# Expert results shared out one step sooner, VectorE's own high part in half blocks, relational groups in pairs

## The chip, the cores and the metric

The kernel runs on one NeuronCore of a Trainium2 chip. Its engines run side by side, each with its own instruction list, and order themselves by semaphores: TensorE (PE in the profile; weight loads are PEld), VectorE (DVE), ScalarE (ACT), GpSimd (POOL) and SyncE (SP), which here only issues DMAs. The metric is the time of one execution on the device in microseconds (us). Three runs of the kernel before took 1425.64, 1419.89 and 1427.88 us.

## What is computed

The input x is 8192 tokens of 128 values (128 graphs of 64 nodes). Four residual layers, each on a layer norm of x, follow one another. Cut to what matters:

```
x = x + L0_gnn(layernorm(x), adj)        # 3 rounds of a gated graph network (GRU cell)
x = x + L0_ffn(layernorm(x))             # 8 experts, hidden 512, relu, top 2 of them
x = x + L1_gnn(layernorm(x), adj)        # relational graph convolution with a sigmoid gate
x = x + L1_ffn(layernorm(x))             # 8 experts, hidden 512, gelu, top 2 of them

def ffn(x):                              # both expert layers have this form
    top_p, top_e = top_2(softmax(x @ Wg + bg))
    for e in range(8):
        h = act(x @ W1[e] + b1[e])       # 128 -> 512
        y = h @ W2[e] + b2[e]            # 512 -> 128
        out += share(top_p, top_e, e) * y
```

## The kernel before

Stages follow one another: opening, gated graph (to about 470 us), first expert stage (names e1..., to about 806), relational stage (names c_..., to about 1058), second expert stage (names e2..., to about 1388), combine. Products in higher precision are split: a value is a high part in f16 and a low part in f16, and a product is three matmuls (lines L205, L206 and L207 of `passes`).

**Expert stages** (`experts`, L1381, called twice). Each token was sent to two slots of a table in DRAM (`slots`), sorted by expert, with a tag (home address, share). The table is worked off in 36 blocks of 512 slots: blocks 0 to 23 have one expert each (whole blocks), blocks 24 to 35 have two halves of 256 slots with an expert each (half blocks: each product and each bias is done twice on half the columns). Buffers come in rings of three (RING = 3). The hidden 512 values are four chunks of 128 (CH = 4). The work of block b:

- SP: `load(b)`, a transposing DMA of the block's rows into `xT`; `read_tags(b)`, a DMA of the tags into `label`. In iteration b of SP's loop it waits until up products of block b are done (`h_ps`), issues `load(b+3)` and then `read_tags(b+2)`, which waits for `homes`.
- TensorE: `up_c(b, c)`, chunk c of the hidden layer into one of four banks; `down_c(b, c)`, the product of chunk c with W2, summed up over the chunks; `turn(b)` (L1547), four transposes of the block's result back to rows.
- ScalarE: `hidden(c)` (L1586), the activation function from the bank into `hf` in f32; `hi(c)` (L1592), the high part of `hf` in f16 into `hs`. Its order is hidden0, hidden1, hi0, hidden2, hi1, hidden3, hi2, hi3.
- VectorE: `lo(c)` (L1605), the low part; `collect` (L1630), the sum of the down products out of the bank, with its bias; `addresses`, four small operations that make home addresses and shares for three blocks at once (L1617 to L1623); `share_out` (L1639), the transposed rows times their share into `ys`.
- GpSimd: four scatters (L1511, indirect DMAs) of a block's rows in `ys` to `results` in DRAM.

Each engine has its own order in a step b. TensorE: up(b+1, 0), down(b, 0), up(b+1, 1), down(b, 1), up(b+1, 2), down(b, 2), up(b+1, 3), down(b, 3), and `turn(b-1)` last. VectorE: collect(b-1); addresses, if b is the last of three; share_out(b-2); lo(b+1, 0) to lo(b+1, 3). After the last step VectorE still has collect(35), share_out(34), share_out(35). Blocks 3 to 20 run in a hardware loop (`Fori`) of three turns with six steps each; the others are written out. At block 2 of the first stage VectorE also makes MASK out of ADJ (L1660), two long operations.

**Relational stage** (`relational`, L1711). 16 groups of four tiles (512 tokens) go through a pipeline of 21 steps s. In step s TensorE turns over the tokens of group s-1 (`turn_a`) and the routing tokens of group s-4 (`turn_b`), makes the routing scores of group s-4 (`scores`), the values of group s-1 (`values`: per two tiles a bank, v = 0 and 1; biases are L1877), and the sums over the neighbours of group s-2. ScalarE copies the turned tokens out of the banks (`turned_a`, L1993, into `xT_a`; `turned_b`, L2006, into `xT_b`). VectorE empties the value banks (L2069), takes the scores in (`scores`, L2141) and chooses experts (`choose`) for a batch of groups. BATCHES says how: group 0, group 1 and then pairs, nine batches. `relational_sends` says how many rows of tokens GpSimd sends to their slots in each step, ahead of and behind its root (L1804), which it computes for the norms; ROUTED = 4 steps lie between a group's norm and its choice.

What VectorE's step looks like in the expert stages:

```
def step(b, j, i, v):
    if not isinstance(b, int) or b:
        collect(b - 1, 1 - v)
    if j == RING - 1:
        addresses(b - j, i)
    if not isinstance(b, int) or b > 1:
        share_out(b - 2, (j - 2) % RING, i - (j < 2), v)
    for c in range(CH):
        if not last(b):
            lo(b + 1, (j + 1) % RING, c)
```

## Time and profile before

| | before |
|---|---|
| median of three runs | 1425.64 us (1419.89 to 1427.88) |
| the profiled execution | 1428.36 us, its span 1426.6 us |
| TensorE busy | 918.1 us (64%), 5850 instructions |
| VectorE busy | 905.9 us (64%), 2456 instructions |
| ScalarE busy | 765.8 us (54%), 1392 instructions |
| GpSimd busy | 733.9 us (51%), 717 instructions |
| granted TensorE clock, mean | 0.787 of full speed |

No engine is busy over two thirds of the span, so the stages have to be read one by one, and in a stage one step by itself: how long it lasts, which engine is never idle in it, and which wait ends last. The chain that the profile follows back from the last instruction stays within the last 2% of the span (combine) and says nothing of the stages.

### The profile page before, as it was taken

The numbers are of one execution on the slowest core, as the hardware profiler recorded it, in microseconds if no ns is written. First come the engines' busy times: TensorE is split into PE (matmuls) and PEld (weight loads), VectorE is DVE, ScalarE is ACT, GpSimd is POOL, SyncE is SP. The second block draws the span as 40 slices with busy tenths as digits, with TensorE's granted clock in tenths as the row PEclk, the third lists the DMA queues.
The fourth block names the chain that finished last, engine by engine and source line by source line (L and its number), as shares of the span: only waits on it lengthen the run. The fifth ranks groups of instructions, "written<-read, shape, count | busy, mean of one in ns | idle before, by whom it ended". The sixth has DMA issues, their size and how long they took to land. (4 is left out here: it accounts for less than half of the span.)

```text
span 1426.6 us, 23103 instructions
## 1 busy us (share of the span) xinstructions
PE 918.1 (64%) x5850; PEld 519.1 (36%) x5851; DVE 905.9 (64%) x2456; ACT 765.8 (54%) x1392; POOL 733.9 (51%) x717
## 2 busy tenths in 40 slices
PE   2368778888862357888787176656432968888820
PEld 1244344444432123434565133323210433346620
DVE  5967799999985345555544367767642645554626
ACT  2476767677762145666565165656431655666710
POOL 3501132876757646556544416567566444655540
PEclk9579999999995679899988555555556998999955
DMA  9233221221201524424221223321131342333209
GB/s 249 90 127 94 77 46 23 59 61 48 59 22 42 136 58 100 91 67 85 64 50 45 71 90 119 104 65 55 32 62 52 87 105 58 84 67 70 61 28 340
DMA packets 199164, 115.62 MB, mean 81 GB/s; under 512 B 155084, under 2 KB 175710, under 8 KB 198528
## 3 DMA queue, kind: packets, MB, share of 16 engines
q1 hardware_dynamic: 169008, 69.54, 20.8%
q0 software_dynamic: 17408, 34.13, 7.4%
q10 hardware_dynamic: 12624, 10.49, 2.8%
q8 instruction: 54, 0.88, 0.3%
q14 instruction: 70, 0.57, 0.1%
HBM read 43.80 MB, written 51.61 MB: 67 GB/s over the span
## 5 line engine op out<-in xcount | busy, mean ns | idle before, releaser
L644 POOL DMA_INDIRECT slots<-ROWS,pos x256 | 265.4, 1037 | 78.5 <-issue 71.4
L1511 POOL DMA_INDIRECT results<-e1ys,e1home x144 | 155.5, 1080 | 136.1 <-DVE e1ys L1639 93.7
L1511 POOL DMA_INDIRECT results<-e2ys,e2home x144 | 151.1, 1049 | 136.2 <-DVE e2ys L1639 93.0
L1586 ACT ACTIVATE e1hf<-psum,VT 128x512 f32<-128x512 f32 (+1 forms) x192 | 104.3, 583 | 151.6 <-PE psum L207 82.0
L1605 DVE SCALAR_TENSOR_TENSOR e1hs<-e1hf,e1hs 128x512 f16<-128x512 f32 x144 | 95.6, 690 | 127.4 <-ACT e1hs L1592 88.9
L1586 ACT ACTIVATE e2hf<-psum,VT 128x512 f32<-128x512 f32 (+1 forms) x192 | 104.8, 582 | 126.0 <-remote 59.1
L1605 DVE SCALAR_TENSOR_TENSOR e2hs<-e2hf,e2hs 128x512 f16<-128x512 f32 x144 | 95.8, 691 | 112.5 <-ACT e2hs L1592 83.0
L1363 POOL TENSOR_TENSOR a_Z<-a_Z,a_H 128x512 f32<-128x512 f32 x48 | 68.2, 1420 | 161.5 <-ACT a_Z L1093 159.2
L205 PE MATMUL psum<-e2hs,W 128*128 128x512 f16 (+1 forms) x192 | 66.7, 347 | 55.9 <-DVE e2hs L1605 25.9
L205 PE MATMUL psum<-a_hT,WHH 128*128 128x512 f16 x144 | 58.8, 408 | 52.5 <-ACT a_Z L1093 48.3
L205 PE MATMUL psum<-e1xT,W 128*128 128x512 f16 (+1 forms) x192 | 67.6, 352 | 38.5 <-DMA e1xT<-slots 16.7
L205 PE MATMUL psum<-e1hs,W 128*128 128x512 f16 (+1 forms) x192 | 67.4, 351 | 35.8 <-DVE e1hs L1605 24.9
L1592 ACT ACTIVATE e1hs<-e1hf 128x512 f16<-128x512 f32 x144 | 86.9, 631 | 0.0
L1592 ACT ACTIVATE e2hs<-e2hf 128x512 f16<-128x512 f32 x144 | 86.7, 631 | 0.0
L205 PE MATMUL psum<-e2xT,W 128*128 128x512 f16 (+1 forms) x192 | 66.7, 348 | 23.4 <-issue 11.0
L1804 POOL TENSOR_TENSOR c_rs<-c_var,mhalf 128x12 f32<-128x12 f32 (+2 forms) x22 | 40.5, 1843 | 79.9 <-DVE c_var L2082 45.1
L207 PE MATMUL psum<-e1xT,W 128*128 128x512 f16 (+1 forms) x192 | 67.7, 353 | 3.3 <-issue 3.2
L206 PE MATMUL psum<-e1hs,W 128*128 128x512 f16 (+1 forms) x192 | 67.5, 352 | 2.7 <-issue 1.7
L206 PE MATMUL psum<-e1xT,W 128*128 128x512 f16 (+1 forms) x192 | 67.5, 351 | 2.7 <-issue 2.7
L207 PE MATMUL psum<-e1hs,W 128*128 128x512 f16 (+1 forms) x192 | 67.4, 351 | 2.7 <-issue 2.5
L207 PE MATMUL psum<-e2xT,W 128*128 128x512 f16 (+1 forms) x192 | 66.5, 346 | 1.6 <-issue 1.5
L206 PE MATMUL psum<-e2xT,W 128*128 128x512 f16 (+1 forms) x192 | 66.5, 346 | 0.4 <-issue 0.4
(363 smaller groups left out, 2643.6 us busy)
## 6 DMA issues: line engine op xcount, KB each, us to landing
c_G<-results SPq DMA_DIRECT2D x32, 256.0 KB
d_G<-results SPq DMA_DIRECT2D x32, 256.0 KB, 5.2
slots<-slots SPq DMA_DIRECT2D x16, 264.0 KB
W<-in_L_ffn_W_dram SPq DMA_DIRECT2D x16, 256.0 KB, 3.4
kept<-a_cut SPq DMA_DIRECT2D x16, 256.0 KB, 2.6
slots<-ROWS,pos POOLq DMA_INDIRECT x256
W<-kept SPq DMA_DIRECT2D x8, 512.0 KB
out_dram<-X ACTq DMA_DIRECT2D x16, 256.0 KB, 7.1
```

Of the source, the lines that this page charges most:

```text
L205: pe.matmul(out, lhs(0), rhs(0), start=start, stop=False, skip_group_check=True)
L206: pe.matmul(out, lhs(0), rhs(1), start=False, stop=False, skip_group_check=True)
L207: return pe.matmul(out, lhs(1), rhs(0), start=False, stop=stop, skip_group_check=True)
L644: pool.indirect_dma_start(out=slots, out_offset=bass.IndirectOffsetOnAxis(ap=k["pos"][:, c, t:t + 1], axis=0), in_=k["ROWS32"][:, t, :], i ...
L1363: pool.tensor_tensor(Z[p % 2][:, :], Z[p % 2][:, :], H[p][:, :], ALU.mult).then_inc(zh_sb, 1)
L1511: pool.indirect_dma_start(out=k["results"][m], out_offset=bass.IndirectOffsetOnAxis(ap=home[:, GT * b + q:GT * b + q + 1], axis=0), in_=ys ...
L1586: t = act.activation(hf[c][:, cols], HB[c][:, cols], func, bias=VT[:, bass.ds(e * CH + b1_col + c, 1)], scale=1 / PS)
L1592: act.activation(hs[j][:, 0, c, :], hf[c][:, :], ACT.Copy, scale=AS).then_inc(h_hi, 1)
L1605: dve.scalar_tensor_tensor(out=hs[j][:, 1, c, :], in0=hf[c][:, :], scalar=AS, in1=hs[j][:, 0, c, :], op0=ALU.mult, op1=ALU.subtract).then_ ...
L1804: pool.tensor_tensor(rstd[s % 4][:, lo:hi], var[s % 2][:, lo:hi], k["mhalf"][:, lo:hi], ALU.pow)\
```

## The change

Three parts.

In both expert stages TensorE does `turn(b-1)` in the middle of step b, behind down(b, 1); VectorE does `share_out(b-1)` in step b, between the low parts of chunks 1 and 2, in place of share_out(b-2) at the step's start; `addresses` comes at the second block of each three, not the third; and SP reads the tags of block b+2 before it waits to load block b+3.

In the steps that prepare half blocks VectorE makes the high part of the last chunk itself (`own_high`, a `tensor_scalar` with its own semaphore), and ScalarE leaves it out. `his_by` counts ScalarE's high parts accordingly.

In the relational stage all groups are routed in pairs (eight batches); sends to the slots start one step later, with eight rows a step; TensorE makes the values of a group's first two tiles (v = 0) ahead of the scores; and ScalarE's turned_b stands ahead of norms_a.

```diff
@@ -1408,6 +1408,7 @@
         y_stored = k["stored"][m]
         h_ps, h_f32, h_hi, h_lo, yT_ps, yT_sb, y_ps, y_sb = (
             sem(n) for n in ("h_ps", "h_f32", "h_hi", "h_lo", "yT_ps", "yT_sb", "y_ps", "y_sb"))
+        own_hi = sem("own_hi")
         counted, listed, tails, match, weight, homes, second_in = (
             sem(n) for n in ("counted", "listed", "tails", "match", "weight", "homes", "second_in"))
         HB = banks[0:4]
@@ -1435,6 +1436,13 @@
             if isinstance(b, int) and b >= FULL:
                 return [(2 * b - FULL + h, slice(h * HALF, (h + 1) * HALF)) for h in range(2)]
             return [(b, slice(0, BLK))]
+
+        def halved(b):
+            return isinstance(b, int) and b >= FULL
+
+        def his_by(b):
+
+            return CH * (b + 1) - (max(0, b + 1 - FULL) if isinstance(b, int) else 0)
 
         def half_rows(buf, h):
             return buf[:, :, :].rearrange("p s n -> p (s n)")[:, h * BLK:(h + 1) * BLK].rearrange("p (s n) -> p s n", s=2)
@@ -1488,6 +1496,8 @@
                     sp.wait_ge(counted, 1)
                 if RING <= b < RING + E:
                     tail(b - RING)
+                if 1 <= b and b + 2 < NBLK:
+                    read_tags(b + 2, rows.pop(b + 2))
                 if b + RING == EARLY:
                     sp.wait_ge(listed, 1)
                     sp.wait_ge(tails, 16 * E)
@@ -1495,8 +1505,6 @@
                 if b + RING < NBLK:
                     sp.wait_ge(h_ps, 4 * b + 4)
                     rows[b + RING] = load(b + RING)
-                if 1 <= b and b + 2 < NBLK:
-                    read_tags(b + 2, rows.pop(b + 2))
 
         @block.gpsimd
         def _(pool):
@@ -1568,8 +1576,8 @@
                         known[:] = [e, who(b + 2)]
                     elif c == 1:
                         known[:] = [e, None]
-                if not isinstance(b, int) or b:
-                    turn(b - 1, 1 - v)
+                    if c == 1 and (not isinstance(b, int) or b):
+                        turn(b - 1, 1 - v)
             rounds(pe, step)
             turn(NBLK - 1, (NBLK - 1) % 2)
 
@@ -1595,13 +1603,23 @@
                 for c in range(1, CH):
                     hidden(c)
                     hi(c - 1)
-                hi(CH - 1)
+                if not halved(b):
+                    hi(CH - 1)
             rounds(act, step)
 
         @block.vector
         def _(dve):
+            def own_high(b, j):
+                c = CH - 1
+                dve.wait_ge(h_f32, CH * (b + 1))
+                dve.tensor_scalar(hs[j][:, 0, c, :], hf[c][:, :], AS, None, ALU.mult).then_inc(own_hi, 1)
+                dve.wait_ge(own_hi, b - FULL + 1)
+
             def lo(b, j, c):
-                dve.wait_ge(h_hi, 4 * b + c + 1)
+                if halved(b) and c == CH - 1:
+                    own_high(b, j)
+                else:
+                    dve.wait_ge(h_hi, his_by(b - 1) + c + 1)
                 dve.scalar_tensor_tensor(out=hs[j][:, 1, c, :], in0=hf[c][:, :], scalar=AS, in1=hs[j][:, 0, c, :],
                                          op0=ALU.mult, op1=ALU.subtract).then_inc(h_lo, 1)
 
@@ -1647,13 +1665,13 @@
             def step(b, j, i, v):
                 if not isinstance(b, int) or b:
                     collect(b - 1, 1 - v)
-                if j == RING - 1:
+                if j == 1:
                     addresses(b - j, i)
-                if not isinstance(b, int) or b > 1:
-                    share_out(b - 2, (j - 2) % RING, i - (j < 2), v)
                 for c in range(CH):
                     if not last(b):
                         lo(b + 1, (j + 1) % RING, c)
+                    if c == 1 and (not isinstance(b, int) or b):
+                        share_out(b - 1, (j - 1) % RING, i - (j < 1), 1 - v)
                 if m == 0 and isinstance(b, int) and b == RING - 1:
                     for h in range(2):
                         half = slice(h * NODES, (h + 1) * NODES)
@@ -1661,8 +1679,7 @@
             rounds(dve, step)
             end = NBLK - 1
             collect(end, end % 2)
-            for b in (end - 1, end):
-                share_out(b, b % RING, b // RING, b % 2)
+            share_out(end, end % RING, end // RING, end % 2)
 
 
 
@@ -1681,16 +1698,16 @@
         sp.dma_start(G[:, c, :, :], rows[:, c, bass.ds(GT * g, GT), :]).then_inc(sem, 16)
 
 
-BATCHES = [(0, 1), (1, 1)] + [(g, 2) for g in range(2, 16, 2)]
+BATCHES = [(g, 2) for g in range(0, 16, 2)]
 ROUTED = 4
 SPLIT = 6
 
 
 def relational_sends(NG):
 
-    first = ROUTED + 1
+    first = ROUTED + 2
     n = NG + ROUTED + 1
-    wanted = [0 if s < first else (8, 6, 2)[s - first] if s < first + 3 else 8 if s < NG else CARRY for s in range(n)]
+    wanted = [0 if s < first else 8 if s < NG else CARRY for s in range(n)]
     early = 2 * GT * (NG - QUAD)
     return [max(min(w, early - sum(wanted[0:s])), 0) for s, w in enumerate(wanted)]
 
@@ -1865,11 +1882,10 @@
                 pe.wait_ge(lo_a, g + 1)
                 turn_over(TAh, tok_a[p]).then_inc(a_ps, 1)
 
-            def values(g, p):
+            def values(g, p, v):
 
                 pe.wait_ge(a_sb, g + 1)
-                for q in range(GT):
-                    v = q // 2
+                for q in range(2 * v, 2 * v + 2):
                     if q % 2 == 0:
                         wait_from(pe, val_sb, 2 * g + v - 1)
                     o = Vv[v][:, q % 2, :, :].rearrange("p s d -> p (s d)")
@@ -1939,10 +1955,12 @@
                     turn_a(s - 1, (s - 1) % 2)
                 if 0 <= s - 4 < NG:
                     turn_b(s - 4)
+                if 0 <= s - 1 < NG:
+                    values(s - 1, (s - 1) % 2, 0)
                 if 0 <= s - 4 < NG:
                     scores(s - 4)
                 if 0 <= s - 1 < NG:
-                    values(s - 1, (s - 1) % 2)
+                    values(s - 1, (s - 1) % 2, 1)
                 if 0 <= s - 2 < NG:
                     neighbours(s - 2, s % 2)
                 b, g, n = chosen_at(s)
@@ -2008,10 +2026,10 @@
             def step(s):
                 if 0 <= s - 1 < NG:
                     turned_a(s - 1, (s - 1) % 2)
+                if 0 <= s - 4 < NG:
+                    turned_b(s - 4)
                 if s < SPLIT:
                     norms_a(s, s % 2)
-                if 0 <= s - 4 < NG:
-                    turned_b(s - 4)
                 if 0 <= s - 2 < NG:
                     v_his(s - 2, s % 2)
                 if SPLIT <= s < NG:
```

## Rows read from the trace of the kernel before

**Rows 1.** Windows, two of each expert stage: us, busy time of each engine, PEclk, DMA

```profile
534.00:683.00 149.00, 122.44 (x572) 57.27 (x573) 86.07 (x152) 92.94 (x164) 87.34 (x81) 0.94 0.39 85
683.00:788.00 105.00, 82.78 (x605) 62.99 (x604) 50.55 (x99) 59.94 (x137) 50.70 (x48) 0.86 0.25 52
1120.00:1276.00 156.00, 126.00 (x575) 58.09 (x574) 83.60 (x148) 93.70 (x164) 84.09 (x80) 0.91 0.35 81
1276.00:1369.00 93.00, 74.50 (x603) 59.93 (x601) 50.97 (x98) 60.42 (x138) 50.57 (x48) 0.92 0.29 62
```

**Rows 2.** Table of waits: engine, line, releaser: us in total, times, longest us

```profile
ACT e2hf L1586 <- remote: 59.1, 14, 14.3
ACT e1hf L1586 <- remote: 57.3, 13, 11.6
```

**Rows 3.** Timeline of a whole step, second stage: start us, us, instruction

```profile
1155.73 0.38 PE L207 MATMUL psum<-e2xT,W 128*128 128x512 f16 x1
...
1156.60 0.60 PE L1547 MATMUL psum<-identf,e2yT 128*128 128x128 f32 x4
1157.04 0.38 PE L205 MATMUL psum<-e2xT,W 128*128 128x512 f16 x1
...
1159.41 0.38 PE L207 MATMUL psum<-e2hs,W 128*128 128x512 f16 x1
...
1161.35 0.38 PE L207 MATMUL psum<-e2xT,W 128*128 128x512 f16 x1
...
1156.25 0.69 ACT L1586 ACTIVATE e2hf<-psum,VT 128x512 f32<-128x512 f32 x1
1156.84 1.14 ACT L1592 ACTIVATE e2hs<-e2hf 128x512 f16<-128x512 f32 x2
...
1157.49 1.29 DVE L1605 SCALAR_TENSOR_TENSOR e2hs<-e2hf,e2hs 128x512 f16<-128x512 f32 x2 [0.53 <-ACT e2hs L1592]
1158.91 0.75 DVE L1630 TENSOR_SCALAR e2yT<-psum,VT 128x512 f32<-128x512 f32 x1
```

**Rows 4.** Timeline of a half step, first stage

```profile
737.27 0.27 PE L207 MATMUL psum<-e1xT,W 128*128 128x256 f16 x1
...
740.98 0.27 PE L207 MATMUL psum<-e1hs,W 128*128 128x256 f16 x1
...
741.04 0.88 DVE L1630 TENSOR_SCALAR e1yT<-psum,VT 128x256 f32<-128x256 f32 x2 [0.67 <-issue]
```

**Rows 5.** Groups by line and form, VectorE: busy us, mean ns of one | idle

```profile
L451 DVE TENSOR_SCALAR WIH<-W 128x384 f16<-128x384 f32 x3 | 1.1, 352 | 0.0
```

**Rows 6.** Timeline at MASK in the first expert stage

```profile
530.01 2.65 POOL L1511 DMA_INDIRECT results<-e1ys,e1home  x1 [0.30 <-issue]
...
530.26 4.58 DVE L1660 TENSOR_SCALAR MASK<-ADJ 64x4096 f16<-64x4096 int32 x2
```

**Rows 7.** Timeline, GpSimd, end of the second expert stage: first and last of twelve

```profile
1370.80 0.98 POOL L1511 DMA_INDIRECT results<-e2ys,e2home  x1 [7.49 <-DVE e2ys L1639]
...
1384.92 0.98 POOL L1511 DMA_INDIRECT results<-e2ys,e2home  x1 [0.31 <-issue]
```

**Rows 8.** Timeline of relational step 10

```profile
929.85 1.02 ACT L1993 ACTIVATE c_xT_a<-psum 128x1024 f16<-128x1024 f16 x1 [4.47 <-remote]
...
929.97 0.75 DVE L2069 SCALAR_TENSOR_TENSOR c_sg<-psum,c_sg 128x256 f32<-128x256 f32 x2
...
931.85 0.19 PE L205 MATMUL psum<-WGATE,c_xT_b 128*128 128x8 f16 x1 [4.44 <-ACT c_xT_b L2006]
...
932.26 0.60 PE L1877 MATMUL psum<-relbias,ones 1*128 1x256 f16 x2
...
934.83 0.60 PE L1877 MATMUL psum<-relbias,ones 1*128 1x256 f16 x2
```

**Rows 9.** Waits of VectorE, relational stage, 854 to 1053 us

```profile
DVE S L2141 <- PE psum L207: 20.3, 10, 3.3
```

**Rows 10.** Groups of VectorE, 850.8 to 854.4 us: one of the routing operations

```profile
L585 DVE TENSOR_TENSOR v_wide<-revidx,ROWS 128x32 f32<-128x32 f32 x1 | 0.2, 193 | 0.0
```

## The prediction

> **What bounds the kernel now.** I read the time per stage first, then one undisturbed step of each kind in the timeline, then the table of waits. The two expert stages are the part that the change rewrites most. Cut at the last down product of a block, the 20 whole-block steps 4 to 23 take 149 us in the first expert stage and 156 us in the second, 7.45 and 7.8 us a step; the 12 half-block steps 24 to 35 take 105 and 93 us, 8.75 and 7.75 us a step [rows 1]. TensorE is busy for 80 to 82% of them and is the engine with most to do, but an undisturbed step is shorter than these means: in the timeline [rows 3] chunk 3 of block 8 is up-projected at 1155.73 and the next one at the same place comes 5.62 us later (1161.35), which is the four transposes' 0.44 us and eight groups of products, one up or down product of a chunk each, at 0.645. The rest are pauses: ScalarE waits 57.3 and 59.1 us, in 13 and 14 pieces, for a releaser that the profile can't name [rows 2]. So an expert step is 5.6 us of TensorE work plus, in some steps, a pause of 4 us or so. GpSimd, with 4 scatters of about 1.28 us (start to start [rows 7]) a block, has room to spare, except at the end of a stage: there 12 scatters stand one behind the other, from 1370.80 to 1385.90.
>
> In the relational stage VectorE sets the pace; what it waits for most is the score product of TensorE, 20.3 us in 10 waits [rows 9].
>
> **Moved transposes and share_out, whole blocks.** TensorE now does turn(b-1) in the middle of step b, behind down(b, 1), and not at its end. Nothing is added to its work, but the transposes wait for collect(b-1), and behind them in TensorE's order stand up(b+1, 2), down(b, 2), up(b+1, 3) and down(b, 3). When does collect finish? The timeline shows the chain of an undisturbed step [rows 3]: the last up product ends at 1155.73 + 0.38 = 1156.11; ScalarE makes the activation (start 1156.25) and then both high parts (end 1157.98), VectorE both low parts (end 1158.78), and collect ends at 1158.91 + 0.75 = 1159.66, which is 3.55 us after the product. In the old order TensorE passes down(8, 1) at 1159.79, so nothing would show. But the transposes (0.44 us, 1156.60 to 1157.04) are no longer ahead of it, so TensorE is there at 1159.35. It waits for collect: 0.31 us, plus about 0.13 for the semaphore (the gap between the product's end and ScalarE's start in this step, 1156.11 to 1156.25). The step becomes a loop of 3.55 + 0.13 + 0.44 + three groups of products at 0.645 = 6.05 us in place of 5.62: plus 0.43. There are 22 such steps in a stage (1 to 22), so 9.5 us. Below, 0, if every one has its slack from elsewhere; above, 1 us a step where ScalarE is still behind after a pause.
>
> **Half blocks, with the high part on VectorE.** The same chain [rows 4]: product end 737.27 + 0.27 = 737.54, collect end 741.04 + 0.88 = 741.92, so 4.38 us, while down(30, 1) ends at 740.98 + 0.27 = 741.25. The old order thus would be 0.67 us short by itself. own_high takes some 0.6 us (of the 1.14 for two high parts [rows 3]) off ScalarE, which isn't last here, and puts a tensor_scalar 128x512 to f16 on VectorE between low parts 2 and 3. No such operation is in the trace; the nearest is the 128x384 at 0.352 us [rows 5], so 0.35 to 0.47 us; I take 0.42, and 0.1 for VectorE's wait on its own semaphore. The two low parts run back to back (1.29 us for both [rows 3]), so it adds its length to the chain: 4.90. Between the ends 737.54 and 741.25 lie the transposes and five groups, 0.654 each; an undisturbed half step is thus 0.44 + 8 x 0.654 = 5.67, and the new loop 4.90 + 0.13 + 0.44 + 3 x 0.654 = 7.4 us: plus 1.75, in 11 steps 19 us. Without own_high it would be plus 1.2. Bounds: 0 (a pause covers it) to 2.4.
>
> A 2-port operation of VectorE can also hold up GpSimd: a scatter that meets the MASK operation takes 2.65 us, not 0.98 [rows 6, 7]. 12 operations of 0.42 us a stage are at most 5 us of GpSimd's time, and GpSimd idles in the half steps; only where it is last would it count, and none of them falls behind the last block. Cost zero. The Trainium skill has this as a rule that speaks against the edit (page "SBUF — State Buffer", section "SBUF: two separate sides": a VectorE operation in a 2-port mode locks GpSimd out of the shared ports, so that it can't write descriptors); by that rule, the trace agrees, and if every lock were on the path the sum would be 10 us longer over both stages, which the idle time in the rows of GpSimd contradicts.
>
> **How much of it shows.** 9.5 + 19 = 28.5 us a stage, 57 for both. 27 of the 70 steps hold a pause [rows 2]. Where the pause falls behind the new place of the transposes, the wait lies inside it. I take half of them so: 57 x (1 - 27/140) = 46 us.
>
> **The end of a stage.** Here the change gains. share_out(33) is done in step 34 and share_out(34) in the middle of step 35, so of the 12 scatters that stood behind the last blocks only 8 are left: 4 x 1.28 = 5.1 us a stage, 10.3 for two. Bounds 0 (if the last steps come later by as much) and 2 x 10.
>
> **Addresses and tag reads.** The four small operations move from step j = 2 to j = 1 of each three, and SP reads the tags of block b+2 before it waits for h_ps, no longer behind the load. SP's order is load, tags, load, tags as before; the one tag read in three that waits for `homes` now stands ahead of the load of one block sooner, and its release comes one step sooner too. The load still has two steps. Zero; if SP came late, up(b+3) would wait: at most 1 us in every third step, 20 us.
>
> **Relational stage.** (a) values for tiles 0 and 1 now go ahead of the scores on TensorE. In step 10 [rows 8] xT_a is there at 929.85 + 1.02 = 930.87 and VectorE has emptied the bank (first of the two value operations from 929.97 on) at about 930.4; the half takes 932.26 to 934.83 = 2.57 us. The scores (0.41 us, 931.85 to 932.26) start not at 931.85 but at 930.95 + 2.57 = 933.5. VectorE waits for them in order, with choose, the shifts and the next mixture queued behind. Its wait per step is 2.57 + 0.41 + 0.3 for two semaphores less its second value operation 0.4 = 2.9 us; in the 13 steps 4 to 16 that have both, 37 us against 20.3 before: plus 17. VectorE has other waits that this can swallow; I take plus 12, between 0 and 20. (b) One routing batch fewer: 19 small operations at about 0.19 us [rows 10] go, and those of the first pair grow by some 0.03 us each: minus 3.0. GpSimd sends 8 and 8 rows in steps 6 and 7, not 6 and 2, and a root stands behind: plus 2.6 at most. I take minus 1.5. (c) turned_b ahead of norms_a acts in steps 4 and 5 alone: zero, within 1 us.
>
> **Sum.** The profiled execution took 1428.4 us, with a span of 1426.6; the median of the runs is 1425.6, 2.7 less. 1428.4 + 46 - 10.3 + 12 - 1.5 = 1474.6, and on the scale of the median 1472.
>
> **Rivals.** *The pauses set the pace* (the one on the other side, not slower). Steps last 7.45 to 8.75 us on average, the new loops 6.05 and 7.4. If the pauses come because TensorE runs at 5.6 us a step, a slower step has fewer of them, and the expert stages keep their length. For: the pauses come once in two to three steps, after fast ones. Against: in the trace a step with a pause is longer by the whole pause, and the next is 5.6 us again. It decides once the pauses shrink by 46 us out of 116. Time: 1425.6 - 10.3 + 12 - 1.5 = 1426; with the wait for scores swallowed too, 1414. *The relational order pays and the chain doesn't bind*: TensorE idles for xT_b in the old order, and with 2.57 us of work put there its own chain to relu is 1 us shorter in 13 steps. With the tails: 1425.6 - 10.3 - 13 - 1.5 = 1401. Against: VectorE, not TensorE, is last there. *Every wait shows in full, with ScalarE behind after pauses*: 1 us in whole steps and 2.2 in half ones, 2 x (22 + 24) = 92: 1425.6 + 92 - 10.3 + 15 = 1522. *The change doesn't do what it says*: scatters of block b-1 would not start before step b+1 if the transposes came so late that share_out slips; then the tails stay and 1482 results.
>
> **Chances.** Forecast, with tails kept or lost, 1440 to 1508: 0.54. Full waits, above 1508: 0.07. Pauses set the pace, 1419 to 1440, most of it within 0.5%: 0.20. Faster (scores swallowed as well, 0.10, or the relational order pays, 0.09): 0.19. 0.5% is 7 us, about what a measurement of this kernel can tell from no change: 1418.5 to 1432.8. So faster 0.20, same 0.16, slower 0.64, the last with the upper end of the pauses' case. The range leaves out the full waits and the faster half of the faster cases: 1412 to 1508; the likeliest case by itself spans 1445 to 1500.
>
> **What would show it.** Right: TensorE idle before its transposes (L1547), released by VectorE's collect, some 0.4 us in whole and over 1 us in half steps; the undisturbed whole step at 6.0 us, the half one at 7.4; VectorE's wait for the scores near 2.9 us in each of 13 steps; 8 scatters behind the last share_out but one. Wrong: steps of 5.6 us still there, or a sum of pauses well under 116 us with expert stages as long as before.

## The result, and the profile after

The changed kernel takes 1448.5 us (median of six runs, 1442.2 to 1455.2), the kernel before beside it 1429.7 us: a ratio of 1.0188, with a 95% interval of 1.0133 to 1.0242. (Ratios leave out runs more than 1.5% above the fastest of the same kernel, so they need not be the quotient of the medians.) So it is slower, by 19 us by the medians and 27 by the ratio; 1472 had been forecast, with 1412 to 1508 as the range. Its profiled execution took 1447.9 us, with a span of 1446.1 (1426.6 before).

The span cut into stages, an expert stage from its first up product to the end of its last scatter, and the relational stage as what lies between the two (each cut read from the timeline of its profile):

| us | before | after | difference |
|---|---|---|---|
| opening and gated graph | 477.2 | 477.2 | 0.0 |
| first expert stage | 327.1 | 322.8 | -4.3 |
| relational stage | 258.7 | 283.4 | +24.7 |
| second expert stage | 322.9 | 322.8 | -0.1 |
| combine | 40.7 | 39.9 | -0.8 |
| span | 1426.6 | 1446.1 | +19.5 |

I had put plus 46 on the longer expert steps, minus 10 on the ends of the expert stages and plus 10 or so on the relational stage. The sign of the total is right, its size is too large, and the places are wrong.

Windows of the changed kernel, cut where those of [rows 1] are, at the last down products of blocks 3, 23 and 35 of each expert stage (us, busy time of each engine, PEclk, DMA share, GB/s):

```profile
547.00:690.00 143.00, 125.32 (x577) 58.51 (x576) 82.94 (x148) 93.84 (x162) 86.62 (x80) 0.94 0.37 85
690.00:791.00 101.00, 73.26 (x596) 60.95 (x594) 55.06 (x111) 54.76 (x124) 49.40 (x50) 0.94 0.26 54
1147.00:1289.00 142.00, 122.54 (x573) 57.19 (x572) 83.29 (x148) 94.50 (x163) 85.72 (x79) 0.96 0.38 85
1289.00:1396.00 107.00, 77.30 (x603) 63.00 (x600) 56.23 (x111) 54.11 (x124) 51.92 (x49) 0.92 0.26 52
```

Whole steps have a mean of 7.15 and 7.1 us, where it was 7.45 and 7.8; half steps 8.4 and 8.9, where it was 8.75 and 7.75. Yet the undisturbed step did become longer, as forecast. The timeline in the second stage, from the transposes of block 9 to those of block 10:

```profile
1193.35 0.66 PE L1555 MATMUL psum<-identf,e2yT 128*128 128x128 f32 x4 [0.38 <-DVE e2yT L1648]
...
1195.57 0.38 PE L207 MATMUL psum<-e2xT,W 128*128 128x512 f16 x1
...
1196.08 0.69 ACT L1594 ACTIVATE e2hf<-psum,VT 128x512 f32<-128x512 f32 x1
1196.67 1.14 ACT L1600 ACTIVATE e2hs<-e2hf 128x512 f16<-128x512 f32 x2
...
1197.38 1.28 DVE L1623 SCALAR_TENSOR_TENSOR e2hs<-e2hf,e2hs 128x512 f16<-128x512 f32 x2
1198.74 0.75 DVE L1648 TENSOR_SCALAR e2yT<-psum,VT 128x512 f32<-128x512 f32 x1
...
1199.54 0.66 PE L1555 MATMUL psum<-identf,e2yT 128*128 128x128 f32 x4 [0.36 <-issue]
```

The product ends at 1195.95, collect at 1199.49, 3.54 us later (forecast 3.55, [rows 3]), and TensorE is idle ahead of its transposes until then (0.36 to 0.38 us). The step is 6.19 us (1193.35 to 1199.54), against 5.62.

What gave the time back stands in the table of waits, whole span:

```profile
PE psum L1555 <- DVE e1yT L1648: 52.3, 27, 12.0
DVE S L2159 <- PE psum L207: 39.9, 15, 3.4
PE psum L1555 <- DVE e2yT L1648: 30.0, 21, 3.1
ACT e2hf L1594 <- remote: 21.9, 4, 15.6
```

The first and third lines are the forecast waits of TensorE for collect. The last answers to [rows 2]: ScalarE's waits for a releaser that isn't named have gone from 59.1 us in 14 pieces to 21.9 in 4 (in the first stage from 57.3 in 13 to 10.1 in one). The second line is VectorE's wait for the scores, 21.7 us before over the same whole span.

An unnamed wait is only one name under which a pause shows. The 12.0 us in the first line ended at 520.73, just behind one of ScalarE's unnamed waits (10.06 us, to 517.12): in the new order TensorE, too, is made to wait by a pause, and under the name of collect. So 116.4 to 32.0 us tells that the pauses became fewer, not by how much; the comparison of the two kinds of chip below does.

Another wait in that line was not in the forecast. In block 2 of the first stage VectorE makes MASK, and collect stands behind it; now the transposes and half of TensorE's step stand behind collect:

```profile
535.07 4.75 DVE L1678 TENSOR_SCALAR MASK<-ADJ 64x4096 f16<-64x4096 int32 x2
539.84 0.75 DVE L1648 TENSOR_SCALAR e1yT<-psum,VT 128x512 f32<-128x512 f32 x1
...
540.72 1.11 PE L1555 MATMUL psum<-identf,e1yT 128*128 128x128 f32 x4 [5.72 <-DVE e1yT L1648]
```

The end of the second expert stage, GpSimd and VectorE (L1648 is collect, L1657 share_out; the first and the last scatter of twelve):

```profile
1390.60 1.45 POOL L1519 DMA_INDIRECT results<-e2ys,e2home  x1 [4.48 <-DVE e2ys L1657]
...
1405.23 0.98 POOL L1519 DMA_INDIRECT results<-e2ys,e2home  x1 [0.31 <-issue]
...
1396.69 0.88 DVE L1648 TENSOR_SCALAR e2yT<-psum,VT 128x256 f32<-128x256 f32 x2 [1.34 <-PE psum L207]
1398.31 0.69 DVE L1657 TENSOR_TENSOR e2ys<-psum,e2share 128x512 f32<-128x512 f32 x1 [0.75 <-issue]
```

From the last collect to the end of the last scatter it is 1396.69 to 1406.21, 9.5 us. Before, the last collect stood at 1370.79, and the last scatter [rows 7] ended at 1385.90: 15.1 us. The gain of 5.6 us is close to the 5.1 of the forecast.

### The profile page after: what moved, and what is told of

Same layout as the page of the kernel before. It is cut to its first block and busy times, and to the rows that moved or that the text cites. A ratio compares the mean times of both kernels' runs of the same rounds, so it can differ in the third digit from the quotient of the medians.

```text
span 1446.1 us, 23094 instructions
## 1 busy us (share of the span) xinstructions
PE 917.6 (63%) x5849; PEld 525.9 (36%) x5850; DVE 912.3 (63%) x2461; ACT 758.3 (52%) x1366; POOL 732.3 (51%) x717
## 3 DMA queue, kind: packets, MB, share of 16 engines
q1 hardware_dynamic: 169008, 69.54, 20.3%
## 5 line engine op out<-in xcount | busy, mean ns | idle before, releaser
L644 POOL DMA_INDIRECT slots<-ROWS,pos x256 | 261.8, 1023 | 78.4 <-issue 72.0
L1519 POOL DMA_INDIRECT results<-e2ys,e2home x144 | 154.1, 1070 | 133.1 <-DVE e2ys L1657 90.7
L1600 ACT ACTIVATE e2hs<-e2hf 128x512 f16<-128x512 f32 x132 | 80.0, 625 | 0.0
L1600 ACT ACTIVATE e1hs<-e1hf 128x512 f16<-128x512 f32 x132 | 79.8, 623 | 0.0
L205 PE MATMUL psum<-e1hs,W 128*128 128x512 f16 (+1 forms) x192 | 66.5, 347 | 11.2 <-issue 4.2
L206 PE MATMUL psum<-e1hs,W 128*128 128x512 f16 (+1 forms) x192 | 66.2, 345 | 0.0
L207 PE MATMUL psum<-e1hs,W 128*128 128x512 f16 (+1 forms) x192 | 65.7, 342 | 0.0
```

The lines of the kernel that those rows point to most:

```text
L205: pe.matmul(out, lhs(0), rhs(0), start=start, stop=False, skip_group_check=True)
L206: pe.matmul(out, lhs(0), rhs(1), start=False, stop=False, skip_group_check=True)
L207: return pe.matmul(out, lhs(1), rhs(0), start=False, stop=stop, skip_group_check=True)
L644: pool.indirect_dma_start(out=slots, out_offset=bass.IndirectOffsetOnAxis(ap=k["pos"][:, c, t:t + 1], axis=0), in_=k["ROWS32"][:, t, :], i ...
L1519: pool.indirect_dma_start(out=k["results"][m], out_offset=bass.IndirectOffsetOnAxis(ap=home[:, GT * b + q:GT * b + q + 1], axis=0), in_=ys ...
L1600: act.activation(hs[j][:, 0, c, :], hf[c][:, :], ACT.Copy, scale=AS).then_inc(h_hi, 1)
```

## Experiments

Theory A: the loss comes from the split values, which hold back the scores; and in the expert stages something hides the longer steps. Its rivals are in the expectations. The first four kernels ran beside a kernel before of 1427.7 us (median of 19 runs, which lie between 1405.1 and 1455.8).

### The relational edits one by one

r_split is the kernel before with one edit:

```diff
-                if 0 <= s - 4 < NG:
-                    scores(s - 4)
                 if 0 <= s - 1 < NG:
-                    values(s - 1, (s - 1) % 2)
+                    values(s - 1, (s - 1) % 2, 0)
+                if 0 <= s - 4 < NG:
+                    scores(s - 4)
+                if 0 <= s - 1 < NG:
+                    values(s - 1, (s - 1) % 2, 1)
```

> The kernel before with one edit of the relational stage alone: the values of a group's first two tiles ahead of the scores. Theory A (the delayed scores, with VectorE standing in wait for them, are the loss): 15 to 25 us slower, the relational stage near 280 us from the last scatter of the first expert stage to the first up product of the second, in place of 259, and VectorE's wait for the scores above 30 us. Rival B (the loss comes from the pairs and the later sends): within 5 us of before. My term for this edit was plus 12, bounds 0 and 20.

1452.5 us, a ratio of 1.0244 (1.0129 to 1.036), as theory A has it. The relational stage is 274.2 us, 15.5 more than before. Its line in the table of waits:

```profile
DVE S L2142 <- PE psum L207: 44.7, 15, 6.1
```

r_pairs is the kernel before with the routing in pairs:

```diff
-BATCHES = [(0, 1), (1, 1)] + [(g, 2) for g in range(2, 16, 2)]
+BATCHES = [(g, 2) for g in range(0, 16, 2)]
-    first = ROUTED + 1
-    wanted = [0 if s < first else (8, 6, 2)[s - first] if s < first + 3 else 8 if s < NG else CARRY for s in range(n)]
+    first = ROUTED + 2
+    wanted = [0 if s < first else 8 if s < NG else CARRY for s in range(n)]
```

> The kernel before with the eight batches of pairs and the sends that go with them, and nothing else. Theory A: minus 1.5 us by my sum, within 4 us of before. Rival B (routing or the sends, now one step later, hold the stage up): 10 us or more slower.

1439.0 us, 1.0156 (1.0039 to 1.0273). By the total alone, 11.3 us over the median beside it, this is rival B. But in its profile the relational stage is 260.1 us, 1.4 more than before, and the one stage that is clearly longer is the second expert stage, which this edit doesn't touch (333.8 us against 322.9, half steps at 8.3 us and not 7.75). r_split, which doesn't touch it either, shows 333.0 there. All four runs of r_pairs also lie between the lowest and the highest of the kernel before. An expert stage can thus differ by 10 us where its code is the same, and the total of one edit of this size can't be read on it; the stage can. Two later kernels with the pairs in them bear this out: r_unsplit below is no slower than e_all, and best, on the other chip, has a relational stage of 242.8 us against 242.3.

e_all is the kernel before with the whole expert part and no relational edit; r_unsplit is the changed kernel with `values` in one piece behind the scores again.

> The kernel before with the whole of the expert part (transposes behind down(b, 1), share_out one step sooner, addresses and tag reads sooner, VectorE's high part in half blocks) and the relational stage untouched. Forecast by my sum: 46 - 10 = plus 36 us. Theory A (undisturbed steps are longer, as forecast, but the pauses shrink by as much): between minus 10 and plus 5 us, with undisturbed whole steps at 6.2 us and not 5.6.

> The changed kernel with one edit undone: all values behind the scores again. Theory A: 15 to 25 us faster than the changed kernel, so 1420 to 1430, level with before or a little under it. Rival B: still 1440 or more. If the edits of the stages are independent, its time is that of the expert part alone and of the pairs alone, added.

e_all: 1422.5 us, 1.0034 (0.9985 to 1.0083). r_unsplit: 1419.95 us, 1.0008 (0.996 to 1.0055). Both medians are 5 to 8 us under that of the kernel before, both ratios a little over 1. So about 28 us of the changed kernel's time go with the one edit (28.5 against its own median, which is from another series of runs; 26 by the difference of the ratios), and the expert part, for which my sum says plus 36, costs nothing that can be measured. If the pairs really cost the 11 us of r_pairs, r_unsplit would stand at 1434; it doesn't. In r_unsplit's profile the relational stage is 254.3 us; in the changed kernel's it is 283.4.

How the edit works is seen in one step of the changed kernel (timeline; L2024 is the copy into xT_b, L2087 VectorE's emptying of a value bank, L1893 the value biases, L2159 the scores on VectorE):

```profile
954.69 1.02 ACT L2024 ACTIVATE c_xT_b<-psum 128x1024 f16<-128x1024 f16 x1
...
955.08 0.75 DVE L2087 SCALAR_TENSOR_TENSOR c_sg<-psum,c_sg 128x256 f32<-128x256 f32 x2
...
955.64 0.58 PE L1893 MATMUL psum<-relbias,ones 1*128 1x256 f16 x2 [5.25 <-DVE c_sg L2087]
...
958.05 0.21 PE L205 MATMUL psum<-WGATE,c_xT_b 128*128 128x8 f16 x1
...
958.60 0.19 DVE L2159 TENSOR_TENSOR S<-psum,c_rs 128x32 f32<-128x32 f32 x1 [2.77 <-PE psum L207]
```

xT_b is there at 955.71, and in the old order the scores would follow at once, as in [rows 8]. Now TensorE first makes values of two tiles, which in turn had to wait for VectorE to empty their bank (xT_a was there at 954.79, TensorE begins at 955.64); the scores start at 958.05, and VectorE, which has had nothing to do since 955.83, stands in wait for 2.77 us. 15 such waits make 39.9 us, 2.66 each.

### The expert edits one by one, on another chip

Four kernels: e_tags is the kernel before with `addresses` at j == 1 and the tag reads ahead of the wait for the load; e_noown is the expert part without own_high; best is the changed kernel with unsplit values and with the transposes and share_out moved to the end of the step; e_turn0 is the expert part with them moved further forward. best and e_turn0 differ from the changed kernel in this place (3 in best, as shown, and 0 in e_turn0, in place of 1):

```diff
-                    if c == 1 and (not isinstance(b, int) or b):
+                    if c == 3 and (not isinstance(b, int) or b):
                         turn(b - 1, 1 - v)
...
-                    if c == 1 and (not isinstance(b, int) or b):
+                    if c == 3 and (not isinstance(b, int) or b):
                         share_out(b - 1, (j - 1) % RING, i - (j < 1), 1 - v)
```

> The kernel before with two small edits of the expert stages alone: addresses at the second block of each three, and the tag reads ahead of the wait for the next load. The transposes stay at the end of TensorE's step and share_out is that of block b-2. I had these at zero. Theory C (the earlier addresses take the wind out of the pauses, and that has paid for the longer steps of the expert part): 30 to 50 us faster than before, undisturbed steps at 5.62 us, ScalarE's waits for a releaser not named well under 116 us. Rival D (the pauses shrink because TensorE's steps are longer): within 6 us of before, pauses as before.

> The expert part without VectorE's high part: transposes behind down(b, 1), share_out, addresses and tags sooner, ScalarE makes all four high parts. My sum: half steps 0.55 us shorter than with it in 11 steps of each stage, so 12 us faster than the whole expert part (1422.5), about 1410. Theory D (something else sets the mean step): within 4 us of the whole expert part, with shortest half steps at 6.9 us, not 7.7.

> The changed kernel without the split values and with the transposes back at the end of TensorE's step (share_out of block b-1 behind the last low part, so 8 scatters are left at the end of a stage, as in the changed kernel). Against the changed kernel with unsplit values (1419.95). My sum says the longer steps cost 46 us in both stages: 1375 to 1395. Theory C: the same, 1375 to 1400. Theory D: 1412 to 1426, with undisturbed whole steps at 5.62 us and pauses as long as before the change.

> The expert part with the transposes still sooner, behind down(b, 0), and share_out behind the first low part. The loop through collect then holds five groups of products: 3.55 + 0.13 + 0.44 + 5 x 0.645 = 7.35 us for an undisturbed whole step, and about 8.7 for a half one. If each longer step shows in full: 22 x 1.3 + 11 x 1.3 = 43 us a stage more than the whole expert part, 1510. Theory D (a mean of 7.2 to 7.5 us for whole steps is set elsewhere): whole steps stay near 7.5 us, half ones near 8.7, together 10 us a stage more at most, 1420 to 1445.

They ran on another chip than the four above, and there the kernel before itself takes 1229.0 us (19 runs, 1226.6 to 1232.6), 200 us less. All absolute numbers expected above therefore miss, and what they were to decide about the pauses (theories C and D) can't be read here; the ratios can:

| kernel | us | ratio to before there |
|---|---|---|
| e_tags | 1229.4 | 1.0008 (0.9994 to 1.0021) |
| best | 1230.1 | 1.0001 (0.9988 to 1.0015) |
| e_noown | 1279.2 | 1.0403 (1.0381 to 1.0425) |
| e_turn0 | 1424.3 | 1.1593 (1.1568 to 1.1617) |

On this chip the pauses don't exist. The windows of e_tags, blocks 4 to 23 and 24 to 35 of the second stage:

```profile
987.00:1099.00 112.00, 112.00 (x571) 57.19 (x570) 84.25 (x148) 96.36 (x164) 87.34 (x80) 1.00 0.48 108
1099.00:1167.00 68.00, 66.19 (x599) 57.92 (x597) 48.02 (x96) 59.92 (x135) 53.06 (x50) 1.00 0.44 85
```

20 whole steps take 112 us, 5.62 each without an exception, TensorE is busy for all of it, and the clock is granted in full; in [rows 1] the same 20 steps take 156 us at 0.91. The table of waits of this kernel has no line with a releaser that isn't named. With no pauses to hide it, the place of the transposes shows in full. TensorE's transposes of e_noown in the half steps of the first stage:

```profile
702.74 0.66 PE L1547 MATMUL psum<-identf,e1yT 128*128 128x128 f32 x4 [1.16 <-DVE e1yT L1630]
...
709.79 0.66 PE L1547 MATMUL psum<-identf,e1yT 128*128 128x128 f32 x4 [1.16 <-DVE e1yT L1630]
```

That is 7.05 us a half step, with 1.16 us of waiting for collect. Whole steps are 6.19 us in e_noown and 7.49 in e_turn0 (expected 7.35), half ones about 10.5 in e_turn0, where I had expected 8.7. The clock is enough to explain the missing 1.8 us: TensorE stands idle for 3 us in each of these steps, and then 15 to 23 of its products run at a granted clock of 0.50 and start 0.1 us further apart. The half steps of the first stage as a whole, one wait for collect, and two stretches of the step that follows it (windows: PEclk is the third number from the right):

```profile
677.00:801.00 124.00, 87.35 (x595) 69.04 (x593) 55.77 (x109) 54.00 (x122) 49.16 (x49) 0.82 0.20 42
732.85 1.11 PE L1554 MATMUL psum<-identf,e1yT 128*128 128x128 f32 x4 [3.37 <-DVE e1yT L1647]
735.30:738.60 3.30, 3.30 (x17) 2.37 (x16) 1.29 (x2) 2.02 (x5) 0.00 (x0) 0.50 0.02 5
738.80:741.50 2.70, 2.70 (x26) 2.26 (x24) 1.03 (x2) 2.15 (x5) 0.98 (x1) 1.00 0.07 24
```

In the slow stretch a product of 256 columns starts every 0.21 us, in the fast one every 0.11. e_noown, whose waits are 1.16 us, keeps a clock of 0.98 to 1.00 in its half steps. My sum for a longer wait had no term for this.

e_noown is 50.2 us slower than the kernel before, from the place of the transposes and of share_out alone (e_tags, with the moved addresses and tags, is level). best has the steps back at 5.62 and the shorter stage ends, and is still no faster: its half steps are 5.85 and 6.05 us on average, against 5.7 in e_tags, two whole steps of its second stage are longer too, and together they eat up the gain at the stage's end (12.6 us from the last collect to the last scatter's end, against 17.2 and 18.4). Which of its edits lengthens the half steps wasn't tried; own_high is one of them.

### The changed kernel on both kinds of chip

> The changed kernel once more, because the kernel before took 1229 us beside the last four kernels and 1428 us beside the first four. On a chip where the kernel before takes about 1229 us and shows no pauses, the longer steps must show in full: whole steps 6.2 in place of 5.62 in 22 steps (13 us a stage), half steps near 7.8 in place of 5.7 in 11 steps (23 us), the tails minus 5 a stage, the split values plus 16 to 29: plus 78 to 91 us, 1307 to 1320. On one where it takes about 1428 us: 1440 to 1455 as measured.

> The whole expert part with the relational stage untouched, once more beside the changed kernel. Where the kernel before takes about 1229 us: 2 x (13 + 23 - 5) = plus 62, 1291. Where it takes about 1428 us: 1415 to 1430 as measured. The difference to the changed kernel is the relational part on the same chip: 16 to 29 us on either.

> The changed kernel with unsplit values and the transposes back at the end of TensorE's step, which was level with before (1230.1 against 1229.0) on a chip where undisturbed steps fill the stages. Where the kernel before takes about 1430 us: Theory D says 1412 to 1430, since what sets the mean step there isn't the chain through collect; my first sum says 1375 to 1395, because the longer steps should show.

> The changed kernel, beside the last. Where the kernel before takes about 1229 us: 1307 to 1320, as expected before. Where it takes about 1430 us: 1440 to 1455.

The first two ran beside a kernel before of 1431.3 us (13 runs, 1412.5 to 1452.5). whole: 1448.9 us, 1.0166 (1.0131 to 1.0201). e_all_again: 1417.1 us, 0.9881 (0.9814 to 0.9948). So the relational edits cost 31.8 us there, a little above the 16 to 29 expected, and the expert part is faster than the kernel before, by 14 us by the medians and 17 by the ratio. With e_all, which was level, that makes 0 to 1.2% for the same kernel.

The other two ran beside one of 1227.4 us, so best_again could not tell what the old place of the transposes, with the shorter stage ends, brings where there are pauses. best_again: 1230.4 us, 1.0022 (1.0012 to 1.0033). whole_again: 1306.1 us, 1.0624 (1.0598 to 1.065): plus 78.7 us, where 78 to 91 had been worked out from the measured steps. Its table of waits, and the half steps of the first stage with own_high (L1615):

```profile
DVE S L2159 <- PE psum L207: 39.3, 15, 2.8
PE psum L1555 <- DVE e1yT L1648: 37.0, 36, 5.0
PE psum L1555 <- DVE e2yT L1648: 33.1, 35, 3.0
```

```profile
701.49 0.42 DVE L1615 TENSOR_SCALAR e1hs<-e1hf 128x512 f16<-128x512 f32 x1
...
703.41 0.88 DVE L1648 TENSOR_SCALAR e1yT<-psum,VT 128x256 f32<-128x256 f32 x2 [0.77 <-issue]
...
704.34 0.66 PE L1555 MATMUL psum<-identf,e1yT 128*128 128x128 f32 x4 [1.70 <-DVE e1yT L1648]
...
711.92 0.66 PE L1555 MATMUL psum<-identf,e1yT 128*128 128x128 f32 x4 [1.69 <-DVE e1yT L1648]
```

A half step is 7.58 us, 0.53 more than without own_high (7.05), with the operation itself at 0.42.

The same kernels on both kinds of chip, stage by stage (each from its profile, steps from the last down product of one block to that of another; for the kernel before on the second kind stands e_tags, which is level with it; none: without pauses):

| us | old steps, pauses | changed, pauses | old steps, none | changed, none |
|---|---|---|---|---|
| mean whole step, stage 1 / 2 | 7.45 / 7.8 | 7.15 / 7.1 | 5.73 / 5.62 | 6.3 / 6.35 |
| mean half step, stage 1 / 2 | 8.75 / 7.75 | 8.4 / 8.9 | 5.7 / 5.7 | 7.55 / 7.45 |
| undisturbed whole step | 5.62 | 6.19 | 5.62 | 6.19 |
| first expert stage | 327.1 | 322.8 | 238.9 | 274.3 |
| relational stage | 258.7 | 283.4 | 242.3 | 254.2 |
| second expert stage | 322.9 | 322.8 | 235.4 | 264.7 |

Without pauses, the expert part costs 35.4 + 29.3 = 64.7 us and the relational part 11.9. With pauses, the expert part costs nothing or gains up to 17, and the relational part costs 25 to 32.

Read across, the table says what the pauses are worth with all that hangs on them: the two expert stages are 88.2 + 87.5 = 175.7 us longer with pauses in the old order, and 48.5 + 58.1 = 106.6 us in the new one. The pauses thus gave back 69 us, where the steps took 65.

## Why the prediction was right, and where it wasn't

**What bounds an expert step.** That an undisturbed step is 5.6 us of TensorE and the rest is pauses was right, and the chip without pauses shows it: 5.62 us a step. What I took for the kernel's own nature, though, belongs to the chip on which it ran. And a pause costs more than the time in which TensorE stands still: TensorE is busy for 126 us in the 20 whole steps of the second stage [rows 1] and for 112 in e_tags, with the same products. So of 44 us, 14 are products at a lower granted clock (0.91 against 1.00), and 30 are idle time.

**Moved transposes.** The chain through collect was right to 0.01 us (3.54 against 3.55), the loop short by 0.14 (6.19 against 6.05): the last up product's row ends 0.16 us after the next product starts (0.38 against the 0.22 from start to start in the timeline), and I had counted the step from starts and the chain from that end. As I had it, 22 x 0.43 = 9.5 us a stage; with the measured step 22 x 0.57 = 12.5.

**Half blocks.** own_high at 0.42 us was right, and so was its place on the chain: 0.53 us a step measured against 0.52 worked out (4.90 against 4.38). The half step is 7.58 us (the terms of the forecast add up to 7.43), without own_high 7.05 (6.91): the same 0.14 to 0.15 again. That ScalarE has one operation less in the step buys nothing: own_high's cost shows in full. Its operations were taken as free for GpSimd, and nothing speaks against that: the scatters take 1.08 and 1.07 us on average in the two stages, 1.08 and 1.05 before.

**How much of it shows: the step that failed.** I took 57 us, less a share of 27/140 for steps in which a pause would cover the wait, 46, which with the ends of the stages is plus 36. The profile with pauses showed minus 4 instead, the one without pauses plus 65. The discount assumed pauses that stay as they are while a wait hides inside some of them. In fact they shrank by about what the steps grew, 69 us against 65. The unnamed waits of ScalarE in the expert stages tell the same of every kernel that ran on a chip with pauses: 116 to 123 us in the three with old steps (the kernel before, r_split, r_pairs), 23 to 51 in the five with the expert part. The rival that I gave 0.20, *the pauses set the pace*, is what happened in these expert stages, and the pauses passed the point of decision that I had named (a loss of 46 of 116 us). Its reason, that pauses come because TensorE runs at 5.6 us a step, isn't shown: on the other chips e_tags runs at 5.62 us a step and has none.

What the pauses are stays open. The trace of the kernel before shows one in the second stage so (ScalarE, the weight loads and the products of TensorE):

```profile
1140.34 0.69 ACT L1586 ACTIVATE e2hf<-psum,VT 128x512 f32<-128x512 f32 x1 [2.49 <-PE psum L207]
1148.59 0.69 ACT L1586 ACTIVATE e2hf<-psum,VT 128x512 f32<-128x512 f32 x1 [7.56 <-remote]
...
1138.64 0.38 PE L207 MATMUL psum<-e2xT,W 128*128 128x512 f16 x1
...
1142.75 0.10 PEld L207 LDWEIGHTS psum<-e2xT,W 128*128 x1
1150.62 0.10 PEld L205 LDWEIGHTS psum<-e2hs,W 128*128 x1 [7.78 <-issue]
```

The product for which ScalarE waits (chunk 1 of block 7) stands at 1138.64, but ScalarE goes on only at 1148.59; by then TensorE has run out of work too. GpSimd's scatters go on through it. The profile models the ends of products, so it can't tell whether they were finished late or whether the word of them came late. The DMA traffic of the kernel is the same on both kinds of chip (199164 packets, 115.62 MB), so it isn't by itself the cause; whether it takes part on the one kind wasn't tried. Why kernels with longer TensorE steps have less of them isn't shown either, only that they do: five profiles with 6.2 us steps have mean whole steps of 7.0 to 7.4 us, three with 5.6 us steps 7.45 to 7.8. All five also have the earlier addresses, tag reads and share_out; which of these edits shrinks the pauses wasn't taken apart where there are pauses. I can't say from this that a mean of about 7.3 us would hold for other loops: e_turn0, meant to show it, ran where there are no pauses.

**The end of a stage.** Near: 5.1 us forecast; 5.6 to 6 measured with pauses, 7 to 8 without.

**Addresses and tag reads.** Zero was right where it could be measured alone (1.0008, with 1.0021 as the upper end). On a chip with pauses they weren't tried alone, and there they may have a part in the smaller pauses.

**Relational stage.** The wait was priced right and then discounted by feel. 13 waits of 2.9 us against 20.3 before gave plus 17; the waits grew from 21.7 to 39.9 us, plus 18.2, 15 of 2.66. I took 12, since VectorE's other waits could swallow some. With pauses that failed: the stage grew by 24.7 us, and by 28 to 32 by r_unsplit and e_all_again. Part of it is again the pauses' (VectorE's unnamed wait for the routing ranks, L630, went from 7.6 to 13.6 us); the rest wasn't taken apart. In particular, the split alone (r_split) lengthens the stage by 15.5 us and the pairs alone by 1.4, which leaves 8 of the 24.7 unexplained. Without pauses 12 hold (11.9), but by luck. VectorE's wait for the scores, and its wait for GpSimd's root, which stands right behind (L2054, in the changed kernel L2072), in e_tags and in whole_again:

```profile
DVE S L2141 <- PE psum L207: 5.8, 4, 2.7
DVE c_shift_a L2054 <- POOL c_rs L1804: 20.3, 13, 3.1
DVE S L2159 <- PE psum L207: 39.3, 15, 2.8
DVE c_shift_a L2072 <- POOL c_rs L1821: 4.8, 5, 1.2
```

There the scores were no wait to speak of before, and the edit added 33.5 us, not 17; 15.5 of them replaced the wait for the root. With pauses the wait for the root was 8.4 us before and 4.8 after, so little could be swallowed. One thing stood otherwise than in the forecast, which had the value bank as free before xT_a (930.4 against 930.87 [rows 8]): in the step shown above it is free after xT_a (955.6 against 954.79), so that TensorE and VectorE stand in wait for each other in one step. The pairs were near enough: minus 1.5 forecast, plus 1.4 in the stage of r_pairs, within what stages differ by.

**The total.** 1472 against 1448.5: right side, within the range, and partly by luck, with two errors of opposite sign: the expert part 36 to 40 us too dear, the relational part 14 to 21 us too cheap. The loss that was measured isn't the one that was forecast: it is the split values, not the longer expert steps. On a chip without pauses the same terms give 57 - 10 + 12 - 2 = 57 without the discount, and 79 was measured. By part, both stages together: the steps up to block 23 grew by 38 us (19 in the sum), the half steps by 44 (38), the ends shrank by 17 (10), the relational stage grew by 12 (10.5), the rest by 2 (0). The 0.15 us a step are some 10 of the missing 22; some 5 are MASK's, in front of collect (blocks 3 and 4 of the first stage take 12.87 + 6.60 us, in e_tags 5.62 + 7.85), which the sum had put at nothing; the others are single longer steps that weren't followed up.

## What to carry to other kernels

Cost a moved step by the loop that it closes: here product, activation, low part, collect, transposes and back, worked out from the rows of one undisturbed step, was right to 0.2 us a step, as long as TensorE's clock held; with 3 us of idle time a step it fell, and the sum was 1.8 us short. Look for long operations, here MASK, ahead of whatever the loop now waits for. Then ask what else sets the mean: where the mean step is a third longer than the undisturbed one and the profile names no releaser for the rest, a longer step may cost nothing. Whether a shorter one then brings anything wasn't tried. Work placed ahead of a small product on which another engine stands in wait lengthens that wait in full; the stage is spared only as much as the next wait of that engine was long, so look up that one before taking anything off.

## What the runs showed of the hardware

The same program takes 1227 to 1229 us on two chips and 1428 to 1431 on at least two others, with runs that agree within 0.5% on the former and spread over 2.4 to 3.6% on the latter. The difference lies in pauses in which other engines go on only long after TensorE's products stand in the profile (in the case shown, 9.6 us after); ScalarE's unnamed waits in the expert stages of the kernel before are 27, from 0.2 to 14.3 us. On the faster kind none of the six profiles has an unnamed wait, and the granted clock in the whole-block steps is 1.00 (e_tags) and not 0.91 to 0.94 [rows 1]. A change can be 6.2% slower on one kind and 1.7% on the other, and the expert part alone is level or 1.2% faster on the one where the same steps cost 65 us on the other. Chips thus have to be told apart before times are compared, by the kernel before beside every run.

TensorE's granted clock went with its idle time within a step: after waits of 3.0 to 3.4 us it stood at 0.50, the lower of its two levels (1.2 GHz), for part of the products that followed (e_turn0), and with waits of 1.16 us it stayed at 0.98 to 1.00 (e_noown).
